# A two-layer block on one core: layer 0 with all transposed tokens kept, four value buffers, keys projected for several batches at once, and a new order on every engine

## The chip, the cores and the metric

One core of one Trainium2 chip. The metric is the device time of one execution in microseconds (us). TensorE (PE) multiplies, VectorE (DVE), ScalarE (ACT) and GpSimd (POOL) do the element work, and SyncE (SP) issues the DMAs. Matmul results land in eight PSUM banks of 512 float32 columns.

## What is computed

Eight batches of 256 tokens with 128 features pass two layers, each an attention-like branch plus a feed-forward branch on the normalised input. Cut to what matters:

```python
x = L0_attn_x                                   # (8, 256, 128)
xn = _layernorm(x)
# layer 0: attention, 16 heads of 8, 4 key/value heads, and a gated expert network
q, k, v = xn @ Wq + bq, xn @ Wk + bk, xn @ Wv + bv
attn = softmax(q k^T / sqrt(8)) ; out = (attn v) @ Wo + bo
ffn  = gates(top 2 of 8 of xn @ Wg) * (relu(xn @ w1) @ w2)
x = x + out + ffn
xn = _layernorm(x)
# layer 1: causal 4-tap convolution, a scan over the tokens of each batch with 16 states, and a
# 4-matrix network (128 -> 512 -> 512 -> 512 -> 128)
xs, z = split(xn @ W_in) ; xs = silu(conv(xs) + conv_b)
dt = softplus(xs @ W_dt + b_dt) ; B = xs @ W_x
h = h * exp(-exp(A_log) * dt) + B ; ys = sum(h) + D * xs      # per state, along the tokens
x = x + (ys * silu(z)) @ W_out + ternary_network(xn)
```

## The kernel before

**Layer 0** works batch by batch (8 batches `b`). The transposed, normalised tokens of a batch stand in one of two buffers `xnT`. `project` multiplies them with Wq and with Wk (tiled four times side by side, so that 128 rows come out, L457 and L460) into the two halves of one bank, ScalarE moves both out with their biases (`qk_out`, L521 and L522), GpSimd splits them into three bf16 parts (`qk_split`, L692 to L695), SyncE writes the parts to memory (`put`) and reads them back laid out by head (`fetch`, `stack`). The scores are made twice: `S` with tokens on the rows, for the maxima that VectorE takes (`M`, L589), and `A` with keys on the rows and the maxima folded in, for the exponentials of ScalarE (`E`, L548). There are 16 of each per batch. Two banks serve `S` and two serve `A`; for the last batch one of the latter goes to layer 1, so its `A` and `E` alternate. `S` uses the lower half of the array's rows and `A` the upper, and a pair placed together overlaps. `pv` multiplies the exponentials with the values (L357, four column tiles of 32 at a time); the values stand in one of two buffers `v_sb`. `heads`, `back` and `proj_out` finish the attention, `v_gate`, `ffn_in`, `ffn_out` and the small steps `G` on GpSimd make the value rows, the gate and the expert branch. `max_rows` transposes the maxima, `negated_maxima`, `maxima_split` and `rows` bring them into the operands of `A`.

**Layer 1** works on four groups `g` of 512 tokens. `x_in` (L933), the taps on ScalarE (L1015), the convolution on VectorE (L1142), `gate_x` and `gate_z` on ScalarE, `step_in` (L953) and `dt` (L1060) feed 32 decays `D` per group on ScalarE (L1088); VectorE runs 32 scans per group (L1163; one `scan` of the order is two of them), each on a row of B that `b` broadcasts (L869); GpSimd adds each scan to `acc` (L1218) and makes `y` (L1226), from which `out` starts (L970). `ffn`, `second` (L896) and `third` (L908) are the network, with `sil`, `gelu` and `hid` on ScalarE. Four buffer pairs `hb` stand between scans and additions, 31 buffers `da` between decays and scans. The start of `acc` for a group (L1210) waits for both `xs` tiles of that group.

**The order** is written out by hand for each engine in the table `ORDERS`, in which `S`, `A`, `scan` and so on are names of pieces, `3*M` is three of them, and the n-th use of a name is the n-th piece of its kind. Every engine runs its list in order; semaphores do the rest. `warm` is a pair of matmuls on ones (L451); there are 44 of them, and nobody reads what they make. A change of ScalarE's function set costs an `ACT_TABLE_LOAD`. The two layers overlap: layer 1 starts while the last two batches of layer 0 are still running.

## Time and profile before

| what | value |
|---|---|
| median of 3 runs | 371.86 us (370.92 to 372.0) |
| span of the profiled execution | 370.3 us |
| mean granted TensorE clock | 0.990 |
| busy: PE, DVE, ACT, POOL | 361.6, 303.1, 314.4, 238.0 us |
| instructions | 5874 |

The span counts from the first to the last instruction; the median lies 1.6 us above it. PE's busy time is modelled: matmuls overlap in the array, and the distance from the start of one to the start of the next is what one costs. A float32 matmul leaves two records, so x4 for `L457` in a row that covers one product of two parts is normal. POOL's 64% is an average over a first half in which it has little to do and a second in which it has no pause.

### The profile page before, as it was taken

The numbers are of one execution on the slowest core, as the hardware profiler recorded it, in microseconds if no ns is written. First come the engines' busy times: TensorE is split into PE (matmuls) and PEld (weight loads), VectorE is DVE, ScalarE is ACT, GpSimd is POOL, SyncE is SP. The second block draws the span as 40 slices with busy tenths as digits, with TensorE's granted clock in tenths as the row PEclk, the third lists the DMA queues.
The fourth block names the chain that finished last, engine by engine and source line by source line (L and its number), as shares of the span: only waits on it lengthen the run. The fifth ranks groups of instructions, "written<-read, shape, count | busy, mean of one in ns | idle before, by whom it ended". The sixth has DMA issues, their size and how long they took to land.

```text
span 370.3 us, 5874 instructions
## 1 busy us (share of the span) xinstructions
PE 361.6 (98%) x1810; PEld 185.9 (50%) x1810; DVE 303.1 (82%) x508; ACT 314.4 (85%) x540; POOL 238.0 (64%) x287
## 2 busy tenths in 40 slices
PE   7999999999999999999999999999999999999996
PEld 6757454546454553433324445465445464464546
DVE  4786879978788888579878768989999989998950
ACT  4934878886988887899998899999999999799870
POOL 2156504642527211342989673999999999999990
PEclk9999999999999999999969999999999999999999
DMA  6477282746265220220000000001000000000000
GB/s 217 125 145 147 93 200 35 174 143 120 58 110 123 43 55 2 52 85 0 1 21 3 1 0 2 0 0 48 5 0 21 0 3 28 1 2 1 0 28 28
DMA packets 29902, 19.63 MB, mean 53 GB/s; under 512 B 4496, under 2 KB 28848, under 8 KB 29616
## 3 DMA queue, kind: packets, MB, share of 16 engines
q1 hardware_dynamic: 29872, 19.26, 21.3%
q8 instruction: 14, 0.23, 0.3%
q14 instruction: 16, 0.13, 0.1%
HBM read 13.69 MB, written 5.37 MB: 51 GB/s over the span
## 4 chain that ended last, share of the span: by engine, by line
PE 68%; ACT 8%; DMA 2%; issue 2%; DVE 2%; SPq 0%; POOL 0%; ACTq 0%; DVEq 0%; POOLq 0%
PE bank L908 15%; PE bank L896 13%; PE bank L357 6%; PE bank L980 4%; PE bank L342 4%; ACT da L1088 3%; PE bank L869 3%; PE bank L885 3%; PE bank L886 3%; PE bank L953 3%; PE bank L933 3%; PE bank L388 2%; PE bank L328 2%; PE bank L396 2%; PE bank L970 2%; ACT pt L548 2%
## 5 line engine op out<-in xcount | busy, mean ns | idle before, releaser
L1218 POOL TENSOR_TENSOR acc<-acc,hb 128x512 f32<-128x512 f32 x128 | 158.1, 1273 | 11.6 <-DVE hb L1163 11.2
L1163 DVE TENSOR_TENSOR_SCAN hb<-da,bank 128x512 f32<-128x512 f32 x128 | 145.9, 1200 | 15.1 <-PE bank L869 9.1
L589 DVE TENSOR_REDUCE mx<-bank 128x2 f32<-128x512 f32 x128 | 83.1, 683 | 16.9 <-PE bank L328 14.4
L1088 ACT ACTIVATE da<-dt,nega 128x510 f32<-128x510 f32 x128 | 82.2, 713 | 0.2
L548 ACT ACTIVATE pt<-bank 128x512 f32<-128x512 f32 x128 | 71.2, 596 | 9.8 <-PE bank L342 8.7
L896 PE MATMUL bank<-sil,ld 128*128 128x512 f32 x128 | 59.1, 595 | 0.0
L908 PE MATMUL bank<-gelu,ld 128*128 128x512 f32 x128 | 58.5, 593 | 0.1
L342 PE MATMUL bank<-q_st,k_st 51*128 51x512 bf16 x128 | 42.2, 386 | 1.8 <-ACT pt L548 1.5
L328 PE MATMUL bank<-k_st,q_st 48*128 48x256 bf16 x240 | 38.9, 273 | 0.1
L896 PEld LDWEIGHTS bank<-sil,ld 128*128 128x128 f32 x128 | 24.3, 192 | 26.3 <-issue 25.7
L908 PEld LDWEIGHTS bank<-gelu,ld 128*128 128x128 f32 x128 | 23.8, 190 | 25.6 <-issue 24.7
L357 PE MATMUL bank<-pt,v_sb 128*32 128x512 f32 x256 | 35.4, 632 | 0.0
L342 PEld LDWEIGHTS bank<-q_st,k_st 51*128 51x128 bf16 x128 | 9.4, 93 | 38.3 <-ACT pt L548 25.5
L869 PE MATMUL bank<-b_parts,sel 96*128 96x512 bf16 x64 | 24.3, 393 | 0.4 <-DVE hb L1163 0.4
L1088 ACT ACT_TABLE_LOAD x18 | 23.1, 1283 | 0.3
L1142 DVE SCALAR_TENSOR_TENSOR xc<-bank,ld,xc 128x510 f32<-128x510 f32 (+2 forms) x24 | 17.6, 743 | 3.5 <-ACT xc L1015 2.9
L328 PEld LDWEIGHTS bank<-k_st,q_st 48*128 48x128 bf16 x240 | 15.5, 94 | 8.5 <-DVE mx L589 4.8
L692 POOL TENSOR_TENSOR qk_parts<-qk,qk_parts 128x512 bf16<-128x512 f32 x7 | 8.1, 1156 | 16.2 <-ACT qk_parts L522 16.2
L388 PE MATMUL bank<-xnT,w 128*128 128x256 f32 x64 | 17.3, 392 | 0.0
L933 PE MATMUL bank<-xnT,ld 128*128 128x512 f32 x32 | 16.7, 607 | 0.5 <-DVE xc L1142 0.3
L980 PEld LDWEIGHTS bank<-ld,gelu 128*128 128x128 f32 x128 | 15.8, 192 | 2.4 <-issue 2.1
L885 PE MATMUL bank<-xnT,ld 128*128 128x512 f32 x32 | 16.5, 598 | 0.0
(148 smaller groups left out, 534.0 us busy)
## 6 DMA issues: line engine op xcount, KB each, us to landing
q_st<-q_scr SPq DMA_DIRECT2D x8, 384.0 KB, 4.9
q_st<-q_scr SPq DMA_DIRECT2D x15, 192.0 KB, 3.8
ld<-in_pack SPq DMA_DIRECT2D x2, 1024.0 KB, 6.3
q_scr<-qk_parts SPq DMA_DIRECT2D x8, 192.0 KB, 2.1
k_st<-k_scr SPq DMA_DIRECT2D x15, 96.0 KB, 4.5
q_scr<-qk_parts SPq DMA_DIRECT2D x8, 128.0 KB, 2.1
out<-x SPq DMA_DIRECT2D x8, 128.0 KB, 1.9
ld<-in_pack SPq DMA_DIRECT2D x1, 968.0 KB, 5.4
```

The source lines that it names most:

```text
L328: last = mm(s_bank[n % 2][:, j * T:(j + 1) * T], q_st[b % 2][0:ROWS, 2 * pair + j, q * P:(q + 1) * P], k_st[b % 2][0:ROWS, 2 * pair // G, ...
L342: mm(st(b, n)[:, :], k_st[b % 2][HALF:, kv, kt * P:(kt + 1) * P], q_st[b % 2][HALF:, h0:h0 + 2, :].rearrange("r h n -> r (h n)"), start=Tr ...
L357: last = mm(pv_bank[kv * VW:(kv + 1) * VW, :], v_sb[b % 2][:, kt, kv, at:at + VW], pt[:, (4 * grp + kv) % 8, :], start=(grp == 0), stop=(g ...
L548: act(pt[:, n % 8, :], st(b, n)[:, :], ACT.Exp, scale=HD ** -0.5).then_inc(p_ok, 1)
L589: eng.tensor_reduce(mx[:, 2 * pair:2 * pair + 2, q], s_bank[n % 2][:, :].rearrange("p (h k) -> p h k", h=2), AX.X, ALU.max).then_inc(mx_ok, 1)
L869: mm(b_bank(g, s)[:, :], sel[:, s, :], b_parts[:, g % 2, :], start=True, stop=True).then_inc(b_ps, 1)
L896: last = mm(f_bank(g, c)[:, :], h1[:, k, c * P:(c + 1) * P], sil[:, k, :], start=(k == 0), stop=(k == KC - 1))
L908: last = mm(f_bank(g, c)[:, :], h2[:, k, c * P:(c + 1) * P], g2[:, k, :], start=(k == 0), stop=(k == KC - 1))
L980: last = mm(out_bank(g, q)[:, r], g3[:, k, r], w3[:, k, :], start=False, stop=(k == KC - 1 and q == out_last(g, q)))
L1088: act(da(n)[:, :, 1:T], dt[:, g % 2, c, :].rearrange("p (b n) -> p b n", b=GB)[:, :, 1:T], ACT.Exp, scale=nega[:, c, s:s + 1]).then_inc(da ...
L1163: eng.tensor_tensor_scan(hb[:, s % NPAIR, c, :], da(n).rearrange("p b n -> p (b n)"), b_bank(g, s)[:, :], 0.0, ALU.mult, ALU.add).then_inc ...
L1218: TT(acc[:, g % 2, c, :], acc[:, g % 2, c, :], hb[:, s % NPAIR, c, :], ALU.add).then_inc(add_ok, 1)
```

## The change

- The transposed tokens of all eight batches are kept: `xnT[b]` is now a slice of the buffer that layer 1 uses for its own transposed tokens. `xn` has two buffers in place of one, `v_sb` four in place of two (cleared one after another by `clear_values`).
- Keys are projected by `project_keys` for the batches (0), (1, 2, 3) and (4, 5, 6, 7) together: each batch's 32 key rows go to a column tile of their own of one bank. `project` makes the queries alone. Copying out, splitting and writing to memory are separate for queries (`q_out`, `split_q`, `put`) and keys (`k_out`, `split_k`, `put_keys`).
- Of the banks, the half `half0` of one is used by `xn_transposes`, `project` and keys of the last group, the half `half1` of another by `v_gate`, `max_rows`, `back` and `proj_out`, and `bB` by the expert branch and `heads`. Who has to have emptied a half before the next one writes it stands in tables of turns (`X_AFTER` to `H_AFTER`).
- The second part of x is 3 batches, not 2, and SyncE issues `head` before it and the constants before the expert weights.
- `scores`' first wait, the fetches and the row DMAs have semaphores for even and odd batches.
- All five lists of `ORDERS` are new.

```diff
+NV = 4
+KEYS = ((0,), (1, 2, 3), (4, 5, 6, 7))
+X_AFTER = "- q0 x1 x2 q1 q2 x5 x6"
+Q_AFTER = "x0 x3 x4 k2 q3 q4 q5 q6"
+KEYS_AFTER = "x7"
+V_AFTER = "- m0 m1 m2 m3 m4 m5 m6"
+M_AFTER = "v0 v1 v2 p1 p2 v5 p4 v7"
+T_AFTER = "v3 p0 v4 v6 p3 m7 h6 h7"
+P_AFTER = "t0 t1 t2 t3 t4 t5 t6 t7"
+F_AFTER = "- f0 f1 h1 h2 f4 h3 h4"
+H_AFTER = "f2 h0 f3 f5 f6 f7 p5 p6"
...
-    xnT = [sb(f"xnT_{p}", [P, T]) for p in range(2)]
-    xn = sb("xn", [P, TPB, P])
+    xnT = [t["xnT1"][:, b * T:(b + 1) * T] for b in range(NB)]
+    xn = [sb(f"xn_{p}", [P, TPB, P]) for p in range(2)]
...
-    v_sb = [sb(f"v_sb{p}", [P, TPB, NKV, VS + VW]) for p in range(2)]
+    v_sb = [sb(f"v_sb{p}", [P, TPB, NKV, VS + VW]) for p in range(NV)]
...
-    X_PARTS = ((0, TPB), (TPB, 3 * TPB), (3 * TPB, NT))
+    X_PARTS = ((0, TPB), (TPB, 4 * TPB), (4 * TPB, NT))
...
         def project(b):
             reached(eng, xnT_ok, b, 1, 1)
-            mm(bA[:, 0:T], wq[:, :], xnT[b % 2][:, :], start=True, stop=True)
+            emptied(eng, Q_AFTER, b)
+            mm(half0, wq[:, :], xnT[b], start=True, stop=True).then_inc(q_ps, 1)
             if b == 0:
-                mm(st_bank[0][:, 0:T], wkx[:, :], xnT[b % 2][:, :], start=True, stop=True)
-            mm(bA[:, T:2 * T], wk4[:, :], xnT[b % 2][:, :],
-               start=True, stop=True).then_inc(qk_ps, 1)
+                mm(st_bank[0][:, 0:T], wkx[:, :], xnT[b], start=True, stop=True).then_inc(kx_ps, 1)
+
+        def project_keys(j):
+            reached(eng, xnT_ok, KEYS[j][-1], 1, 1)
+            if j == 1:
+                eng.wait_ge(k_ok, 1)
+                eng.wait_ge(k_split, 1)
+            if j == 2:
+                emptied(eng, KEYS_AFTER, 0)
+            for i, b in enumerate(KEYS[j]):
+                last = mm(key_bank(j)[32 * i:32 * i + 32, :], wk4[:, 0:NKV * HD], xnT[b], start=True, stop=True)
+            last.then_inc(k_ps, 1)
...
-        def qk_out(b):
+        def q_out(b):
             eng.wait_ge(ld_cst, 16)
-            reached(eng, qk_ps, b, 1, 1)
-            reached(eng, split, b - 1, 3, 3)
-            reached(eng, scr_ok, b - 1, 16 * NSTK, 16 * NSTK)
-            for half, bias in ((0, bq_c), (1, bk_c)):
-                c = slice(half * T, (half + 1) * T)
-                if b > 0:
-                    act(qk[:, c], bA[:, c], ACT.Identity, bias=bias[:, 0:1])
-                last = act(qk_parts[:, 0, c], bA[:, c], ACT.Identity, bias=bias[:, 0:1])
-            last.then_inc(qk_ok, 1)
+            reached(eng, q_split, b - 1, 3, 3)
+            reached(eng, scr_ok, b - 1, 16 * NRUN, 16 * NRUN)
+            reached(eng, q_ps, b, 1, 1)
+            if b > 0:
+                act(qk[:, 0:T], half0, ACT.Identity, bias=bq_c[:, 0:1])
+            act(qk_parts[:, 0, 0:T], half0, ACT.Identity, bias=bq_c[:, 0:1]).then_inc(q_ok, 1)
...
-    vector="""ones moments inverse moments inverse v_out first_split M moments 5*M inverse M gate_sum M gate_norm 4*M
+    vector="""ones moments inverse moments clear_values inverse moments 2*first_split M v_out 3*M clear_values inverse
```

TensorE at the start of the program. L451 and L500 are the warm matmuls, L444 and L493 the transposes of batch 0, L457, L459, L460 and L507, L509, L519 the projections, L317 and L376 the first scores. Before:

```order
1 L451 MATMUL bank<-warm_in 128x256 x18
2 L444 MATMUL bank<-head,xn 128x128 x2
3 L451 MATMUL bank<-warm_in 128x256 x8
4 L457 MATMUL bank<-xnT,head 128x256
5 L459 MATMUL bank<-xnT,head 128x256
6 L460 MATMUL bank<-xnT,head 128x256
7 L388 MATMUL bank<-xnT,w 128x256 x2
```

After:

```order
1 L500 MATMUL bank<-warm_in 128x256 x40
2 L493 MATMUL bank<-head,xn 128x128 x2
3 L500 MATMUL bank<-warm_in 128x256 x8
4 L507 MATMUL bank<-xnT,head 128x256
5 L509 MATMUL bank<-xnT,head 128x256
6 L519 MATMUL bank<-xnT,head 32x256
7 L500 MATMUL bank<-warm_in 128x256 x2
```

Forty warm matmuls in place of 18 stand ahead of the first transpose, and the key product has 32 columns of weights.

TensorE around the last scores of batch 7. L342 and L403 are `A`, L357 and L418 `pv`, L953 and L1029 `step_in`, L869 and L944 `b`, L408 and L462 `back`, L414 and L469 `proj_out`, L896 and L971 `second`, L432 `heads`. Before:

```order
396 L869 MATMUL bank<-b_parts,sel 128x512
397 L953 MATMUL bank<-xs,ld 128x512 x2
398 L342 MATMUL bank<-q_st,k_st 128x512
399 L869 MATMUL bank<-b_parts,sel 128x512
400 L342 MATMUL bank<-q_st,k_st 128x512
401 L414 MATMUL bank<-cst,oT 128x128 x2
402 L342 MATMUL bank<-q_st,k_st 128x512 x2
403 L869 MATMUL bank<-b_parts,sel 128x512
404 L342 MATMUL bank<-q_st,k_st 128x512
405 L357 MATMUL bank<-pt,v_sb 32x512 x8
406 L869 MATMUL bank<-b_parts,sel 128x512 x2
407 L896 MATMUL bank<-sil,ld 128x512 x4
```

After:

```order
395 L403 MATMUL bank<-q_st,k_st 128x512
396 L418 MATMUL bank<-pt,v_sb 32x512 x4
397 L1029 MATMUL bank<-xs,ld 128x512 x2
398 L944 MATMUL bank<-b_parts,sel 128x512
399 L403 MATMUL bank<-q_st,k_st 128x512
400 L462 MATMUL bank<-head,on 128x128 x2
401 L403 MATMUL bank<-q_st,k_st 128x512
402 L418 MATMUL bank<-pt,v_sb 32x512 x4
403 L944 MATMUL bank<-b_parts,sel 128x512
404 L403 MATMUL bank<-q_st,k_st 128x512
405 L469 MATMUL bank<-cst,oT 128x128 x2
406 L418 MATMUL bank<-pt,v_sb 32x512 x4
```

A `pv`, a `step_in` and a `back` that stood ahead of the last four `A` now stand between them, and the last two `pv` no longer stand together.

VectorE at the turn from group 1's scans to group 2's. L1142 is the convolution and L1129 and L1205 the product for `zs`, both of group 3; L1125 and L1201 are the products for `sil` of group 2's network; L1163 and L1239 are scans. Before:

```order
215 L1142 SCALAR_TENSOR_TENSOR xc<-bank,ld,xc 128x2x253
216 L1163 SCALAR_TENSOR_TENSOR hb<-da,bank 128x512 x2
217 L1125 SCALAR_TENSOR_TENSOR sil<-bank,ld,sil 128x512
218 L1129 SCALAR_TENSOR_TENSOR zs<-zs,bank 128x512
219 L1125 SCALAR_TENSOR_TENSOR sil<-bank,ld,sil 128x512
220 L1163 SCALAR_TENSOR_TENSOR hb<-da,bank 128x512 x4
221 L1129 SCALAR_TENSOR_TENSOR zs<-zs,bank 128x512
222 L1125 SCALAR_TENSOR_TENSOR sil<-bank,ld,sil 128x512 x2
```

After:

```order
229 L1239 SCALAR_TENSOR_TENSOR hb<-da,bank 128x512 x6
230 L1201 SCALAR_TENSOR_TENSOR sil<-bank,ld,sil 128x512 x2
231 L1205 SCALAR_TENSOR_TENSOR zs<-zs,bank 128x512 x2
232 L1201 SCALAR_TENSOR_TENSOR sil<-bank,ld,sil 128x512
233 L1239 SCALAR_TENSOR_TENSOR hb<-da,bank 128x512 x2
234 L1201 SCALAR_TENSOR_TENSOR sil<-bank,ld,sil 128x512
235 L1239 SCALAR_TENSOR_TENSOR hb<-da,bank 128x512 x8
```

Five products in place of three stand ahead of the second pair of scans of group 2.

ScalarE at the turn from group 0's scans to group 1's. L1015 and L1091 write the tapped input, L1022 and L1098 are `zs` and L1109 `xs`, all of group 2; L1009 and L1085 are `sil` of group 1's network; L1118 makes the normalised rows of group 3; L1088 and L1164 are decays of group 1. Before:

```order
234 L1015 ACTIVATE xc<-bank,ld 128x512
235 L1088 ACT_TABLE_LOAD
236 L1088 ACTIVATE da<-dt,nega 128x2x255
237 L1015 ACTIVATE xc<-bank,ld 128x512
238 L1088 ACTIVATE da<-dt,nega 128x2x255
239 L1009 ACT_TABLE_LOAD
240 L1009 ACTIVATE sil<-bank,ld 128x512
241 L1022 ACTIVATE zs<-bank 128x512
242 L1009 ACTIVATE sil<-bank,ld 128x512
243 L1022 ACTIVATE zs<-bank 128x512
```

After:

```order
222 L1091 ACTIVATE xc<-bank,ld 128x512 x2
223 L1085 ACT_TABLE_LOAD
224 L1085 ACTIVATE sil<-bank,ld 128x512
225 L1118 ACTIVATE xn<-x,nmean,rstd 128x128 x4
226 L1085 ACTIVATE sil<-bank,ld 128x512
227 L1109 ACTIVATE xs<-xc 128x512
228 L1098 ACTIVATE zs<-bank 128x512 x2
229 L1085 ACTIVATE sil<-bank,ld 128x512
230 L1109 ACTIVATE xs<-xc 128x512
231 L1085 ACTIVATE sil<-bank,ld 128x512
232 L1164 ACT_TABLE_LOAD
233 L1164 ACTIVATE da<-dt,nega 128x2x255 x16
```

Two decays of group 1 that stood between the taps now stand behind all four `sil`, with one table load less. Over the whole program ScalarE's list holds 40 table loads in place of 49.

## Rows read from the trace of the kernel before

**Rows 1.** The page: the granted clock in 40 slices, tenths of full speed.

```profile
PEclk9999999999999999999969999999999999999999
```

**Rows 2.** Stretch, us, busy PE, PEld, DVE, ACT, POOL, clock, DMA share, GB/s.

```profile
154.40:188.10 33.70, 32.14 (x122) 11.86 (x124) 27.16 (x35) 33.15 (x55) 19.05 (x19) 0.96 0.12 38
...
184.00:186.00 2.00, 1.24 (x6) 0.48 (x5) 2.00 (x3) 2.00 (x4) 1.94 (x4) 0.83 0.00 0
186.00:192.00 6.00, 5.85 (x22) 1.41 (x22) 3.42 (x7) 5.35 (x9) 5.44 (x6) 0.50 0.12 33
...
229.00:361.60 132.60, 132.60 (x463) 67.74 (x461) 119.47 (x117) 125.53 (x171) 130.72 (x112) 1.00 0.03 10
```

**Rows 3.** Timeline of PE: start us, us, what, count, at five places.

```profile
35.02 0.39 PE L342 MATMUL bank<-q_st,k_st 51*128 51x512 bf16 x1
...
153.05 1.45 PE L953 MATMUL bank<-xs,ld 128*128 128x512 f32 x3
...
186.92 0.61 PE L342 MATMUL bank<-q_st,k_st 51*128 51x512 bf16 x1 [0.15 <-ACT pt L548]
...
216.05 1.88 PE L933 MATMUL bank<-xnT,ld 128*128 128x512 f32 x4
...
361.97 1.95 PE L970 MATMUL bank<-wout_half,y 128*128 128x128 f32 x16
```

**Rows 4.** Timeline of PE, the start.

```profile
1.36 3.62 PE L451 MATMUL bank<-warm_in 128*128 128x256 bf16 x18 [1.36 <-DVE warm_in L558]
...
5.99 1.04 PE L451 MATMUL bank<-warm_in 128*128 128x256 bf16 x8
...
7.30 0.59 PE L459 MATMUL bank<-xnT,head 128*128 128x256 f32 x2
7.73 0.59 PE L460 MATMUL bank<-xnT,head 128*128 128x256 f32 x2
```

**Rows 5.** Timeline of DVE: statistics of part 2 of x, batch 0's split.

```profile
4.55 0.87 DVE L569 BATCH_NORM_STATS2 bst<-x_sb 128x6 f32<-128x128 f32 x4
...
10.03 0.88 DVE L662 SCALAR_TENSOR_TENSOR qk_rest<-bank,cst,qk_parts 128x256 f32<-128x256 f32 x2
```

**Rows 6.** DMA issues: KB each, median us to landing.

```profile
q_st<-q_scr SPq DMA_DIRECT2D x15, 192.0 KB, 3.8
...
x_sb<-in_x SPq DMA_DIRECT2D x1, 640.0 KB, 6.5
```

**Rows 7.** Timeline of ACT: group 0's `dt`, the last `E`.

```profile
154.44 1.28 ACT L1060 ACT_TABLE_LOAD   x1
...
187.56 0.60 ACT L548 ACTIVATE pt<-bank 128x512 f32<-128x512 f32 x1
```

**Rows 8.** The chain that ended last: start us, us, what.

```profile
109.70 1.85 PE bank L357 x16
...
187.53 3.57 PE bank L357 x16
191.10 0.97 PE bank L869 x2
```

**Rows 9.** Groups by line: busy us, mean ns of one, idle before.

```profile
L1088 ACT ACTIVATE da<-dt,nega 128x510 f32<-128x510 f32 x128 | 82.2, 713 | 0.2
```

**Rows 10.** Timeline of POOL in the second half.

```profile
228.96 2.51 POOL L1218 TENSOR_TENSOR acc<-acc,hb 128x512 f32<-128x512 f32 x2
231.93 8.65 POOL L1218 TENSOR_TENSOR acc<-acc,hb 128x512 f32<-128x512 f32 x7 [0.46 <-DVE hb L1163]
...
359.13 2.49 POOL L1226 TENSOR_TENSOR y<-acc,zs 128x512 f32<-128x512 f32 x2
```

**Rows 11.** Timeline of DVE: group 2's second pair of scans first.

```profile
275.83 4.54 DVE L1163 TENSOR_TENSOR_SCAN hb<-da,bank 128x512 f32<-128x512 f32 x4
```

**Rows 12.** Timeline of ACT: `zs`, then the second `sil` of group 2.

```profile
273.89 0.59 ACT L1022 ACTIVATE zs<-bank 128x512 f32<-128x512 f32 x1
274.44 0.69 ACT L1009 ACTIVATE sil<-bank,ld 128x512 f32<-128x512 f32 x1
```

More of the change, by code:

```diff
@@ L119 @@
-    gpsimd="""ones G qk_split G biased 6*G qk_split maxima_split 6*G biased 2*G qk_split maxima_split 6*G maxima_split
-        qk_split 3*G biased 7*G maxima_split qk_split 8*G maxima_split qk_split 7*G maxima_split G qk_split G
-        constants 7*G shifted maxima_split 8*G maxima_split split 2*start 3*add start 9*add split 9*add start 7*add
-        shifted 4*add 2*y start 9*add split 23*add start 2*y 2*add start 2*add split add start 27*add 2*y 32*add 2*y""",
+    sync="""x_in head x_in constants0 ffn_weights x_in put_keys 3*put 2*put_keys fetch stack 2*put_keys put put_keys
+        2*put fetch put 3*rows stack 2*put fetch rows loads 2*rows 2*put put_keys stack put loads fetch put_keys put
+        put_keys 2*put 3*rows fetch put stack put rows put loads 2*rows fetch put stack 2*put 3*rows fetch stack
+        3*rows loads stack 3*put fetch 4*rows stack 2*rows 2*b_rows out b_rows 3*out b_rows 4*out landed""",
@@ L123 @@
+    gpsimd="""biased ones biased G split_k split_q 7*G split_q maxima_split 6*G split_k 2*G maxima_split split_q 3*G
+        split_q 4*G maxima_split G split_q 7*G biased maxima_split 9*G split_q maxima_split 8*G maxima_split 7*G
+        split_q G shifted maxima_split 4*G constants 4*G maxima_split 2*start split 5*add split 3*add start 20*add
+        shifted add start 2*add y add y start 3*add start 8*add split 21*add 2*y 8*add start split 5*add start 21*add
+        2*y 30*add 2*y""",
 )
@@ L214, in layer0, with score_bank, score_free, group_of @@
     LAST = NB - 1
+    NS3 = LAST * NH
     def head_bank(b):
-        return bA if b < LAST - 1 else bC
+        return bB if b < LAST - 1 else bX
     def st(b, n):
         return st_bank[n % 2 if b < LAST else 0]
+    def score_bank(b, n):
+        return s_bank[n % 2]
+    def score_free(eng, b, n):
+        reached(eng, mx_ok, b, NH, n - 1)
+    def group_of(b):
+        return next(j for j, batches in enumerate(KEYS) if b in batches)
+    def key_bank(j):
+        return half0 if j == 2 else st_bank[1][:, 0:T]
+    EMPTIED = dict(x=((xnT_ok, 1),), q=((q_ok, 1),), k=((k_ok, 1),), v=((v_ok, 1), (srt_ok, TPB)), m=((negm_ok, 1),),
+                   t=((oT_ok, 1),), p=((x1_ok, 1),), h=((on_ok, 1),), f=((y_ok, 1),))
+    def emptied(eng, before, n):
+        name = before.split()[n]
+        if name == "-":
+            return
+        for signal, per in EMPTIED[name[0]]:
+            eng.wait_ge(signal, per * (int(name[1:]) + 1))
+        if name == "q0":
+            eng.wait_ge(q_split, 1)
+            eng.wait_ge(kx_ok, 2)
     def x_part(b):
@@ L302, in ffn_weights @@
             eng.dma_start(w12[:, :], a["w12"]).then_inc(ld_ffn, 16)
-        return dict(x_in=x_in, head=head, constants0=constants0, ffn_weights=ffn_weights, put=put, fetch=fetch, rows=rows,
+        return dict(x_in=x_in, head=head, constants0=constants0, ffn_weights=ffn_weights, put=put, put_keys=put_keys, fetch=fetch, rows=rows,
                     stack=stack, loads=loads)
@@ L1283, in program @@
         early = early_buffers(sb)
[L1284 removed]
+        t["hb"], t["dt"], t["xnT1"] = early["hb"], early["dt"], early["xnT1"]
         with ExitStack() as only0:
```

326 lines of the change are left out of this document (172 added, 154 removed).

## Prediction

> **What bounds the kernel now.** The profiled execution spans 370.3 us and the median is 371.86, so 1.56 us lie around the span. I read the page's rows by slices first. The clock row [rows 1] has one slice at six tenths, a little past the middle, and full speed everywhere else. Then PE's timeline at the places where the program changes character [rows 3] cuts the span into five: 35.02 us to the first `A`; 118.03 to the first `step_in` of layer 1 (153.05), in which PE's pieces follow each other; 33.87 to the last `A` (186.92); 29.13 to the first `x_in` of group 2 (216.05); 145.92 from there to the last group's `out0` (361.97), and 8.3 behind it.
>
> The table of stretches [rows 2] says who is full in each. In 154.4 to 188.1 ScalarE is busy 33.15 of 33.70 us: the last exponentials and the decays of group 0 lie one behind the other, and PE waits for them now and then (busy 1.24 of 2 us in 184 to 186, granted clock 0.83 there). Then the clock is 0.50, the lower of its two levels (1.2 of 2.4 GHz), from 186 to 192, exactly where both last `pv` lie: 16 records took 3.57 us, and 1.85 in the middle of the program [rows 8]. That cost is on the path, because behind the last `A` PE is full again. In 229.0 to 361.6 GpSimd is busy 130.72 of 132.60 us and PE 132.60: the additions end in `y` at 361.62 [rows 10], `out0` starts at 361.97. Two engines bound this part together, so a gain on PE alone brings nothing there.
>
> **The change, part by part.**
>
> *Key products.* A product of 256 columns costs 0.43 us from start to start [rows 4]; before there are eight of them for `S`'s keys, 3.44 us. After there are three groups of one, three and four column tiles. Column tiles placed together already stand in the program: 16 records of `pv`, that is two pieces of four tiles with 512 columns, take 1.85 us [rows 8], 0.93 each, 0.46 with 256 columns; with 0.08 for entering and leaving it is 0.54 a group. Bounds: 0.43 (no such cost) and 1.72 for four tiles that don't run together (4 x 0.43). I take 0.54, since `pv` is the same form. Five of the eight products (batches 3 to 7) stood behind the first `A`, on the full stretch of PE; one group of four replaces them: 2.15 - 0.54 = **1.6 us less**. The other two groups lie at the start, where PE waits and fills with warm matmuls. The wider split on GpSimd and ScalarE's ten copies fewer lie beside PE's work and cost nothing there.
>
> The Trainium skill ("TensorEngine Tiling (Array Packing)", Key Properties) says that a change of tiling mode drains TensorE. No row here shows a drain by itself. By that rule, with the 0.16 us by which a record of 0.59 outlasts its distance of 0.43 [rows 4] paid once in and once out, my estimate would be 0.3 us less gain.
>
> *Start.* The first 18 warm matmuls take 3.62 us (0.20 each), and once the clock is up eight take 0.87 (5.99 to 6.86, 0.11 each) [rows 4]. Twenty-two more ahead of the first transposes cost at most 22 x 0.11 = 2.4 us behind 4.98, which puts these at about 7.4 in place of 5.72. Against this, PE's wait for the `head` load goes, `head` and the constants are issued earlier, and ahead of the first `A` PE's list is stretched with warm matmuls that fill waits. VectorE now has the statistics of the third part of x ahead of batch 0's split, which started at 10.03 [rows 5]. That part is issued near 3 us, and a load of 640 KB took 6.5 [rows 6], so it lands near 9.5 (it is 512 KB now); eight statistics at 0.22 [rows 5] and their means end near 12. Batch 0's queries and keys then come some 2 us later, but their `A` stands at 35. What could be late is batch 1: its first `S` needs the joint keys of batches 1 to 3. The tokens of batch 3, their keys' product, copy, split and three writes come first; counting these in the lists I place the fetch near 25, and with its 3.8 us [rows 6] the keys land at 28.9, about when the first scores that read them are due. Bounds for the first `A`: 34.0 (the waits for the loads go and nothing is late) and 38. I take **35.0, no change**.
>
> *First `A` to `step_in`.* 118.0 less the 1.6 of the keys, less 0.4 for a `proj_out` (four records of 128 columns) that now stands behind the last `A`: **116.0**. The other banks and buffers in turns change who waits, but waits here are of the kind of the 0.15 us ahead of the last `A` [rows 3]; a dozen more or fewer of them bound it at -2 to +2, and I take nothing.
>
> *`step_in` to the last `A`.* ScalarE bounds it and its set of work there is the same (a table load 1.28, an `E` 0.60 [rows 7]). **33.9, no change.** PE has more between its last `A`'s now: a `pv`, a `step_in` and a `back`, about 0.93 + 0.86 + 0.22 us. These fill ScalarE's time, not the path's.
>
> *Last `A` to `x_in`.* Before, two `pv` and two `b` run here at half clock: 3.57 + 0.97 us [rows 8] in place of 1.85 + 0.48. If PE is kept busy between the last `A`'s the clock stays up: 2.2 less. One `pv` (0.93) and one `b` (0.22) are ahead of the last `A` now, a `proj_out` (0.44) comes behind it: 0.7 less. The last `pv` must wait for the last `E`, which started 0.64 us behind its `A` and took 0.60 [rows 3, 7]; the products ahead of it last 0.66, so 0.7 more. 29.1 - 2.2 = **26.9**. Bounds: 26.2 (no wait) and 29.1 (the half clock stays).
>
> *`x_in` to the last `out0`.* Before, the first addition of group 1 starts 12.9 us behind `x_in` (228.96 - 216.05) [rows 3, 10], because two decays stand between the taps. After, all decays come behind the last `sil`. PE feeds it with 12 products of 512 columns at 0.86 (twice 0.43) and two `b` of 0.22, 10.8 us; then `sil` 0.6, table load 1.28 [rows 7], a decay 0.71 [rows 9], a scan 4.54/4 = 1.14 [rows 11], and 0.4 from engine to engine: **14.9**. From there GpSimd's work is the same: 132.66 us to the end of `y` (361.62) less its own idle 1.35 is 131.3. One new wait comes: group 2's second pair of scans stood 59.8 us behind `x_in` [rows 11]; now five products are ahead. Its second `sil` is ready 58.4 behind `x_in` [rows 12], the third `sil` and the products of both `zs` come four PE products later: 58.4 + 3.5 = 61.9, the first result at 63.0, while GpSimd, which before took the result of 60.9 at once, is free at 60.9 + 2.0 (its later start) - 1.35 (its idle) = 61.6. With a product for `sil` between this pair and the next (0.5) that is **1.9**. 14.9 + 131.3 + 1.9 = **148.1**, against 145.9. Bounds: 144.2 (no later start, no new wait) and 150. ScalarE's nine table loads fewer (11.5 us) and PE's gain don't count here, GpSimd's chain ends last.
>
> *Behind `out0`*: 8.3, as before.
>
> Sum: 35.0 + 116.0 + 33.9 + 26.9 + 148.1 + 8.3 = 368.2 of profile, and with 1.56 **369.8 us**.
>
> **The rivals.**
>
> *B, the half clock stays.* ScalarE still sets the distance of the last `A`'s, and PE still waits for it. In the profile the clock fell behind a stretch in which PE was busy 1.24 of 2 us [rows 2]; the 2.0 us of added work stand nearer to the end than those gaps, which may be elsewhere now. Then the 2.2 are not won: 369.8 + 2.3 = 372.1, no measurable change. The Trainium skill ("TensorE: Matmul & The Clock Gate", Part 1) says that TensorE falls back to half speed after idling. The trace agrees in this place, but also ran at half speed while PE was mostly busy.
>
> *C, GpSimd's chain doesn't grow.* If the first addition comes as early as before, or the five products before the second pair find their data sooner, up to 2.2 go: 367.6. For it: VectorE is busy 119.47 and ScalarE 125.53 of these 132.60 us [rows 2], so both could come earlier. Against it: PE's products come one every 0.86 us and the lists are fixed.
>
> *D, a late start, slower than before.* Place: the first scores of batch 1. They wait for the keys of batches 1 to 3 to be projected, copied, split in three parts, written (three DMAs), and read back. Behind them on PE stand all scores that feed VectorE's maxima. It decides once the fetch lands later than 28.9 us; each us costs one. The 2 us of delay of the split on VectorE, if they reach it, and one more for the third batch's transposes, give 3.4: 373.2. For it: the third part of x lands near 9.5 and VectorE's queue stands on it. Against it: before, these waits were covered by warm matmuls.
>
> *E, the end.* PE has no work left while `y` is awaited if GpSimd alone is late by 2 us; before, `third` ended just there. If the clock falls then, the last 5.4 us of PE's work double: 375.2.
>
> *F, the change's key tiles don't run together*: (1.72 - 0.54) on the path and 1 more at the start: 372.0.
>
> **Chances.** Forecast 0.38, B 0.22, C 0.17, D 0.15, E 0.05, F 0.03. A measurement of this kernel can tell 0.3% from no change, that is below 370.7 or above 373.0 us. The forecast's own range (368.6 to 371.0) lies mostly below: 0.31 faster, 0.07 same. C all faster; B 0.02 faster, 0.16 same, 0.04 slower; D 0.02 same, 0.13 slower; E slower; F 0.02 same, 0.01 slower. Sum: faster 0.50, same 0.27, slower 0.23. The range takes in C with its bound and D, and leaves E and the far side of D out: 366.8 to 374.2.
>
> **What would show it.** First `A` at 34 to 36 us, and PE's idle before batch 1's scores put down to a DMA if D. One group of four key tiles taking about 0.54 behind the first `A`. First `step_in` at 151. No slice under nine tenths in the clock row past the middle, and the last `pv` at about 0.93 us; if it takes 1.8, B. GpSimd's first `acc<-acc,hb` of group 1 at 14.9 behind `x_in`, its idle in front of group 2's second pair 1.4 and more; if GpSimd's time from first addition to `y` is 131, C. `third` should end before `out0` starts; a long `out` at the end would be E. What would make all this wrong is a wait in the 116 us of PE's pieces: buffers of values, the banks in turns and the new order of the maxima change every piece's neighbours there, and I have priced them at nothing.

## The result

The changed kernel takes 385.89 us (median of 4 runs, 381.58 to 387.27) against 371.49 for the kernel before (370.92 to 372.0): a ratio of 1.037, 95% interval 1.031 to 1.043. It is slower by 14.4 us. The prediction was 369.8 us with a range of 366.8 to 374.2, so it was wrong in sign and far outside its range. The profiled execution spans 383.1 us; against the forecast for it, 368.2, 14.9 us have to be found.

The same five places on PE as in [rows 3], in the profile of the changed kernel (start us, us, line and operation, what ended the idle before it):

```profile
35.41 0.38 PE L403 MATMUL bank<-q_st,k_st 51*128 51x512 bf16 x1
...
160.95 1.45 PE L1029 MATMUL bank<-xs,ld 128*128 128x512 f32 x3
...
194.88 0.39 PE L403 MATMUL bank<-q_st,k_st 51*128 51x512 bf16 x1
...
223.39 1.09 PE L1009 MATMUL bank<-xnT,ld 128*128 128x512 f32 x2
...
373.11 2.84 PE L1046 MATMUL bank<-wout_half,y 128*128 128x128 f32 x16 [3.55 <-POOL y L1303]
375.74 4.59 PE L1056 MATMUL bank<-ld,gelu 128*128 128x128 f32 x32
```

They give this table, in us:

| stretch | before | forecast | after | miss |
|---|---|---|---|---|
| start to first `A` | 35.0 | 35.0 | 35.4 | +0.4 |
| to the first `step_in` | 118.0 | 116.0 | 125.5 | **+9.5** |
| to the last `A` | 33.9 | 33.9 | 33.9 | 0.0 |
| to group 2's `x_in` | 29.1 | 26.9 | 28.5 | +1.6 |
| to the last group's `out0` | 145.9 | 148.1 | 149.7 | +1.6 |
| behind it | 8.3 | 8.3 | 10.0 | +1.7 |

Two thirds of the miss lie in one stretch, the 118 us of PE's pieces that I had called full and priced for its keys alone. The page of the changed kernel shows the place (busy tenths and granted clock in 40 slices of 9.6 us):

```profile
PE   8999999959999999999999999999999999999967
...
PEclk9999999985999999999999999999999999999998
```

The ninth slice of PE is half empty, and the clock is low in the same slice and the next. The slice at six tenths that [rows 1] has past the middle is gone, and the very last slice, at eight tenths, is new. By stretches, with the columns of [rows 2]:

```profile
80.00:82.00 2.00, 1.98 (x16) 0.52 (x15) 2.00 (x7) 1.55 (x3) 0.00 (x0) 1.00 0.87 217
82.00:84.00 2.00, 0.08 (x4) 0.00 (x0) 0.62 (x4) 0.22 (x1) 0.81 (x4) 1.00 0.94 352
84.00:86.00 2.00, 0.00 (x0) 0.00 (x0) 0.00 (x0) 0.00 (x0) 0.00 (x0) 0.50 1.08 182
86.00:90.00 4.00, 3.87 (x20) 1.08 (x20) 1.69 (x3) 1.99 (x4) 0.00 (x0) 0.50 0.11 18
90.00:94.00 4.00, 3.65 (x15) 2.19 (x16) 3.51 (x9) 1.80 (x4) 0.20 (x1) 0.50 0.00 0
```

From 84 to 86 none of the four compute engines works at all, while the DMA engines are busy throughout (the share of 1.08 counts them as full) and the clock has fallen to its lower level, 1.2 GHz. It stays there until 94.2, 10.2 us in all, though PE is busy again from 86.1. What the DMA engines do can be read from the timeline of SyncE's queue:

```profile
77.94 0.51 SPq L330 DMA_DIRECT2D q_st<-m_parts  x1
78.50 0.58 SPq L289 DMA_DIRECT2D q_scr<-qk_parts  x1
79.11 0.43 SPq L348 DMA_DIRECT2D ld<-in_pack  x1
79.65 1.14 SPq L330 DMA_DIRECT2D q_st<-m_parts  x2
80.88 0.53 SPq L309 DMA_DIRECT2D k_st<-k_scr  x1
```

and PE's timeline has behind the gap, first of all, an `A`:

```profile
86.13 0.58 PE L403 MATMUL bank<-q_st,k_st 51*128 51x512 bf16 x1 [4.05 <-issue]
```

`L348` is `loads`, 1 MB of weights for layer 1, and `L330` is `rows`, 8 KB each, the maxima that the first `A` of batch 3 needs. The change's SyncE list has `rows put loads 2*rows`. The load landed at 85.22 us; the last two rows, issued at 79.65 and 80.26, landed at 84.66 and 86.04. The profile names no releaser for this stop (`<-issue`); that it is the last row follows from its landing 0.09 us ahead of the `A`, and the two experiments that move this load bear it out. Of the 24 row DMAs the trace gives the landing times so (all of the changed kernel; in the kernel before the longest is 2.2 us):

```profile
DMA to landing us min/median/max: 1.8/1.8/5.8
```

Two more rows stand behind a load: that of 559 KB issued at 46.57 landed after 3.6 us, and the rows issued 0.6 and 1.2 us behind it took 3.1 and 3.0 us. PE waits 0.47 us there, up to the first `A` of batch 1 at 50.81.

### The profile page after: what moved, and what is told of

Its sections match the earlier page's. It is cut to its first block, busy times and chain, and to the rows that moved or that the text cites. A ratio compares the mean times of both kernels' runs of the same rounds, so it can differ in the third digit from the quotient of the medians.

```text
span 383.1 us, 5851 instructions
## 1 busy us (share of the span) xinstructions
PE 367.0 (96%) x1810; PEld 185.0 (48%) x1810; DVE 303.2 (79%) x514; ACT 299.0 (78%) x521; POOL 231.7 (60%) x293
## 4 chain that ended last, share of the span: by engine, by line
PE 49%; issue 26%; ACT 8%; DVE 7%; POOL 7%; DMA 3%; SPq 0%; POOLq 0%; ACTq 0%; DVEq 0%
PE bank L418 6%; PE bank L403 5%; POOL acc L1295 4%; DVE hb L1239 4%; PE bank L983 4%; PE bank L446 3%; PE bank L387 3%; PE bank L971 3%; ACT da L1164 3%; PE bank L500 3%; PE bank L454 2%; PE bank L1056 2%; PE bank L1009 2%; PE bank L960 2%; DMA q_scr<-qk_parts 2%
## 5 line engine op out<-in xcount | busy, mean ns | idle before, releaser
L1239 DVE TENSOR_TENSOR_SCAN hb<-da,bank 128x512 f32<-128x512 f32 x128 | 145.4, 1200 | 10.1 <-ACT da L1164 5.7
L1164 ACT ACTIVATE da<-dt,nega 128x510 f32<-128x510 f32 x128 | 81.1, 711 | 0.1
L971 PE MATMUL bank<-sil,ld 128*128 128x512 f32 x128 | 59.6, 594 | 0.3 <-ACT gelu L1145 0.3
L983 PE MATMUL bank<-gelu,ld 128*128 128x512 f32 x128 | 58.4, 593 | 0.7 <-ACT gelu L1145 0.7
L403 PE MATMUL bank<-q_st,k_st 51*128 51x512 bf16 x128 | 42.9, 393 | 5.9 <-issue 4.8
L387 PE MATMUL bank<-k_st,q_st 48*128 48x256 bf16 x240 | 41.1, 281 | 0.5 <-DVE mx L654 0.4
L418 PE MATMUL bank<-pt,v_sb 128*32 128x512 f32 x256 | 35.0, 619 | 0.0
L971 PEld LDWEIGHTS bank<-sil,ld 128*128 128x128 f32 x128 | 23.6, 190 | 22.6 <-issue 21.8
L403 PEld LDWEIGHTS bank<-q_st,k_st 51*128 51x128 bf16 x128 | 9.4, 94 | 37.5 <-ACT pt L613 19.7
L944 PE MATMUL bank<-b_parts,sel 96*128 96x512 bf16 x64 | 24.0, 382 | 0.2 <-DVE hb L1239 0.2
L1056 PEld LDWEIGHTS bank<-ld,gelu 128*128 128x128 f32 x128 | 17.2, 202 | 3.7 <-issue 3.5
L1056 PE MATMUL bank<-ld,gelu 128*128 128x128 f32 x128 | 17.4, 284 | 0.0
L1152 ACT ACTIVATE gelu<-bank,ld 128x512 f32<-128x512 f32 x16 | 10.5, 686 | 7.9 <-PE bank L983 7.7
L1009 PE MATMUL bank<-xnT,ld 128*128 128x512 f32 x32 | 16.6, 614 | 0.1
```

Of the source, the lines that this page charges most:

```text
L387: last = mm(score_bank(b, n)[:, j * T:(j + 1) * T], q_st[b % 2][0:ROWS, 2 * pair + j, q * P:(q + 1) * P], k_st[b % 2][0:ROWS, 2 * pair // ...
L403: mm(st(b, n)[:, :], k_st[b % 2][HALF:, kv, kt * P:(kt + 1) * P], q_st[b % 2][HALF:, h0:h0 + 2, :].rearrange("r h n -> r (h n)"), start=Tr ...
L418: last = mm(pv_bank[kv * VW:(kv + 1) * VW, :], v_sb[b % NV][:, kt, kv, at:at + VW], pt[:, (4 * grp + kv) % 8, :], start=(grp == 0), stop=( ...
L971: last = mm(f_bank(g, c)[:, :], h1[:, k, c * P:(c + 1) * P], sil[:, k, :], start=(k == 0), stop=(k == KC - 1))
L983: last = mm(f_bank(g, c)[:, :], h2[:, k, c * P:(c + 1) * P], g2[:, k, :], start=(k == 0), stop=(k == KC - 1))
L1056: last = mm(out_bank(g, q)[:, r], g3[:, k, r], w3[:, k, :], start=False, stop=(k == KC - 1 and q == out_last(g, q)))
```

## Experiments

All times are compared with the changed kernel's 385.89 us and with runs of the kernel before on the same chip.

**Two loads behind the rows.** The SyncE list of the changed kernel:

```diff
-... fetch rows loads 2*rows 2*put ...  rows put loads 2*rows fetch put stack
+... fetch 3*rows loads 2*put ...  rows put 2*rows fetch loads put stack
```

> The changed kernel with the 1 MB weight loads of batches 1 and 3 issued behind the three row DMAs (and behind the fetch) and not between them. Theory (in the changed kernel the row DMAs of 8 KB issued at 79.65 and 80.26 us landed at 84.66 and 86.04, behind the load issued at 79.11 that landed at 85.22, and the first A of batch 3 started at 86.13): that A starts near 82, PE's stop of 4.05 us and the 10.2 us of half clock behind it go, 8.5 to 10 us less, about 376.5. Rival (the joint keys or the banks in turns hold batch 3 up): the stop stays, and the time is within 1 us of 385.9.

Measured: 382.73 us (379.46 to 385.19); the profiled execution spans 377.7, the shortest of four. In it batch 3's first `A` starts at 83.58, and the stop at 82 is gone. But the gain of the median is 3.2 us (4.6 without the longest of the four executions), not 9, so the expected time is missed, and another stop stands earlier, in PE's timeline:

```profile
58.71 0.39 PE L403 MATMUL bank<-q_st,k_st 51*128 51x512 bf16 x1 [2.37 <-ACT pt L613]
```

ScalarE's timeline has just ahead of it:

```profile
57.23 0.47 ACT L576 ACTIVATE qk<-bank,cst 128x256 f32<-128x256 f32 x1 [3.18 <-DMA q_scr<-qk_parts]
```

`L576` is ScalarE's copy of batch 4's queries. It waits for the last `put` of batch 3's queries, issued at 51.79 behind a load and the `stack` of batch 2 and landed at 57.07; the exponentials stand behind it on ScalarE, `A` behind those on PE. The two longest of the four executions (384.17 and 385.19) have mean clocks of 0.982 and 0.978, the two shorter ones 0.995 and 0.987. So the clock was low for longer in the long ones; that it fell at this stop is not shown, since in the one trace it stays at 1.00 here.

**The mirror image in the kernel before.**

```diff
-... 3*put fetch loads 3*rows 3*put ...
+... 3*put fetch rows loads 2*rows 3*put ...
```

> The kernel before with one weight load moved from behind a fetch to between the first and the second row DMA of batch 3, as the change has it. Theory: the last two rows land behind the load, the first A of batch 3 starts 3 to 4 us later than 81.0, and the whole is 3.5 us longer, up to 8 if the clock halves there. Rival (something of the new kernel alone makes the stop): no change, 371.5.

Measured: 375.92 us against 371.28, ratio 1.0125 (1.011 to 1.014), 4.6 us slower. In PE's timeline the release is named:

```profile
83.69 0.58 PE L342 MATMUL bank<-q_st,k_st 51*128 51x512 bf16 x1 [2.69 <-DMA q_st<-m_parts]
```

A stop of 2.69 us and 3.41 us of half clock (from 83.5), from one moved DMA. So the stop goes when the load is taken away from the rows, and comes, with its releaser named, when a load is put there.

**The stop filled.** 36 matmuls with zero weights stand ahead of batch 3's first `A`:

```diff
+            if n >= NWARM:
+                eng.wait_ge(warm_ok, 2)
+                for _ in range(2):
+                    mm(pv_bank[:, 0:256], zeros[:, :], warm_in[:, P:3 * P], start=False, stop=False)
+                return
```

> The changed kernel with 18 pairs of 128x256 bf16 matmuls with zero weights (nothing is added by them) ahead of the first A of batch 3, where PE stands for 4 us. Theory: the A still starts near 86, the half clock of 10.2 us doesn't come, and the time is 4.5 to 5.5 us less, about 381. Rival (the stop alone costs the 9 us): no change, 385.9.

Measured: 381.71 us (381.13 to 381.85), 4.2 us less, a little under what was expected, and the four executions agree within 0.7 us, where the changed kernel's differ by 5.7. PE's timeline:

```profile
81.71 4.10 PE L483 MATMUL bank<-warm_in,zeros 128*128 128x256 bf16 x36
85.74 0.39 PE L384 MATMUL bank<-q_st,k_st 51*128 51x512 bf16 x1
```

and by stretches:

```profile
86.00:90.00 4.00, 3.49 (x33) 1.23 (x28) 3.55 (x7) 2.88 (x6) 0.00 (x0) 1.00 0.04 7
```

The `A` comes hardly earlier (85.74 for 86.13), but the clock stays at 1.00. The profiled executions can be split: from the first `A` to the first `step_in` this kernel takes 122.23 us (35.34 to 157.57), the changed one 125.54, and e11_second_load_earlier below, which has no stop, 118.03. So the stop costs 4.2 us there and the low clock 3.3, 7.5 together; the 4.2 us between the medians contain executions in which the clock was low for longer.

**Two decays early again,** as in the kernel before, against the change's ScalarE and VectorE lists:

```diff
-... hid 2*taps sil normalise sil ... 16*D      ... 2*mul 2*zm 2*mul 4*scan
+... hid taps D taps D sil normalise sil ... 14*D   ... 2*mul 2*zm scan 2*mul 3*scan
```

> The changed kernel with two decays of group 1 between its taps and their scans ahead of two sil products, as before the change. Theory: GpSimd's first addition of group 1 comes 13 us behind x_in and not 15.3, and since GpSimd's chain ends last, the time is 2 us less, 383.9. Rival (the later waits of GpSimd take it up, or ScalarE's further table load costs it): no change within 0.5 us.

Measured: 385.63 us. The first addition does come 13.0 us behind `x_in` (235.97 - 222.99), but `x_in` to `out0` takes 150.7 us, not less than 149.7: at 276.56 GpSimd waits 1.95 us in place of 0.54. The rival holds; the late first addition was not what this stretch hung on. The order of layer 0 is the changed kernel's, and its stop is there again: PE stands 4.22 us and the clock is low for 3.4 us (86.8 to 90.2), where the changed kernel's profiled execution has 4.05 and 10.2.

**All three loads at their old places.**

```diff
-... 3*rows stack 2*put fetch rows loads 2*rows 2*put put_keys stack put loads fetch ...
+... 3*rows loads stack 2*put fetch 3*rows loads 2*put put_keys stack put fetch ...
-... rows put loads 2*rows fetch put stack ...
+... rows put 2*rows fetch loads put stack ...
```

> The changed kernel with all three weight loads of layer 0 issued at the places of the kernel before: one behind the rows of batch 0 (near 34 us, not 46), one behind the rows of batch 1 (near 48), one behind the fetch of batch 4. Moving two of them alone left two 1 MB loads within 5 us of each other, a put issued at 51.79 landed at 57.07, and ScalarE's query copy, which waits for it, held the exponentials and PE by 2.4 us. Theory (the queue of loads is the cause of both stops): no stop over 1 us in layer 0, first A of batch 3 at 81 to 82, first step_in at 152 to 153.5, time 374 to 376 and the runs within 1.5 us of each other. Rival (the query copy waits for its put whatever the loads do): the stop near 56 us stays, 378 to 383.

Measured: 383.68 us (382.58 to 387.59), the rival's stop and a time just above its range. In the profiled execution, the longest of the six (385.5 us of span), ScalarE's copy waits for its `put` 5.55 us and PE stops for 4.74, and then the clock stays halved for 17 us:

```profile
60.41 0.61 PE L403 MATMUL bank<-q_st,k_st 51*128 51x512 bf16 x1 [4.74 <-ACT pt L613]
```

The load of 968 KB at 47.50 stands ahead of the whole row of small writes now, and the change's list has the third `put` behind the `stack`. Old places in a new list are not the old order.

**The products of `y` last.** In the last group PE adds the network's products (32 records) first, and those of `y` (16) last:

```diff
+            if g == NG - 1:
+                if n < KC + 1:
...
+                        last = mm(out_bank(g, q)[:, r], g3[:, k, r], w3[:, k, :],
+                                  start=(k == 0 and q == out_first(g, q)), stop=False)
+                    return
+                reached(eng, y_ok, g, CI, CI)
...
+                        last = mm(out_bank(g, q)[:, r], y[:, c, r], wo[:, c, :], start=False,
+                                  stop=(c == CI - 1 and q == out_last(g, q)))
```

> As e5_loads_as_before, and in the last group the products of the network (32 records) ahead of those of y (16 records) in PE's list and in the bank. Theory (at the end PE stands 3.6 us for y, the clock halves, and the network's 3.6 us of products come behind y): behind y only the 16 records remain, at full clock; 4.5 to 5.5 us less than e5_loads_as_before. Rival (the network's products wait for their own operand, or the residual and the output DMAs set the end): less than 2 us.

Measured: 377.75 us (376.89 to 380.40), 5.9 less than 383.68 and a little more than expected. The profiled executions show it at the place itself: from the start of `y`'s products to the end of the span it is 10.0 us in e5_loads_as_before (375.50 to 385.5) and 4.8 here. In the changed kernel PE stood 3.55 us for `y` and then ran at half clock (first section). Here it is busy to the end:

```profile
370.15 3.73 PE L1044 MATMUL bank<-ld,gelu 128*128 128x128 f32 x32
373.72 2.00 PE L1053 MATMUL bank<-wout_half,y 128*128 128x128 f32 x16
```

**The pair of scans ahead of `zs`.**

```diff
-... 3*scan 2*mul 2*zm mul scan mul 4*scan
+... 3*scan 2*mul scan 2*zm 2*mul 4*scan
```

> As e6_y_last, and on VectorE the second pair of scans of group 2 behind two products for sil, ahead of both products for zs. Theory (this wait of GpSimd, 1.80 us at 285.8 in the changed kernel, is the cost of the new order of the second half): GpSimd takes the pair 1 to 2 us earlier, 1 to 1.8 us less. Rival (the pair waits for its decays or its row of B, or GpSimd loses the time again before the end): within 0.4 us of e6_y_last.

Measured: 379.79 us (378.25 to 380.38), no gain. GpSimd's wait of 1.80 us goes, and two others of 1.25 and 1.27 us come instead. VectorE waits for a row of B from PE there:

```profile
292.32 2.33 DVE L1263 TENSOR_TENSOR_SCAN hb<-da,bank 128x512 f32<-128x512 f32 x2 [1.44 <-PE bank L944]
```

So in this trace PE's list holds it, not the order on VectorE; no run moves PE's `b` to test that.

**The same turn in the kernel before.** The edit of e6_y_last.

> The kernel before with the same turn of the last group's output products as e6_y_last. There PE finishes third when y is ready, so the network's products (3.59 us) would stand ahead of y's: if GpSimd's y is what ends last, they fit only into time in which PE waits, and PE had none there. Theory (both engines end together at 361.9): the sum on PE stays the same and the gain is under 1 us: 371. Rival (PE's list has slack of its own in the second half that this order uses): up to 3.6 us less, 368.

Measured: 371.12 us against 371.60, ratio 0.999 (0.997 to 1.001): no difference, as the theory has it. PE's work is the same, and there it never stood for `y`.

**SyncE's list sorted.** The first and the third load stand as in e5_loads_as_before. Further, batch 3's third `put` goes ahead of the `stack`, and the second load goes down the list, from 47.50 to 67.36 us:

```diff
-... 3*rows stack 2*put fetch rows loads 2*rows 2*put put_keys stack put loads fetch put_keys put
+... 3*rows loads stack 2*put fetch 3*rows 2*put put_keys put stack fetch put_keys put
-... fetch put stack put rows put loads 2*rows fetch put stack
+... fetch put stack put loads rows put 2*rows fetch loads put stack
```

> The changed kernel with SyncE's list alone altered: as in e5_loads_as_before, and further the third put of batch 3's queries ahead of the stack of batch 2, and the second weight load 18 us later. In e5_loads_as_before that put was issued at 51.51, behind 288 KB of stack and a load, landed at 58.76, and ScalarE's query copy waited for it 5.55 us with the exponentials behind it. Theory (a small DMA behind a large one in the queue holds up what needs it): the put is issued near 50 with no load ahead within 15 us and lands within 2.5 us, ScalarE's wait is under 1 us, no half clock in layer 0, first A of batch 3 at 81 to 82, first step_in at 152.5 to 153.5, and with the tail as it is 374.5 to 376. Rival (the put is held by the copies and splits ahead of it, not by the queue): the stop near 56 us stays and the time is over 380.

Measured: 384.28 us, and a miss, though the stop at 56 us is gone: `A` of batch 2 starts at 63.70, earlier than before the change (64.66). The wait has moved to the load that I had put off:

```profile
75.13 0.20 ACT L1175 ACTIVATE f_half<-ld 128x4 f32<-128x4 f32 x1 [6.75 <-DMA ld<-in_pack]
```

The change prepares layer 1's constants on ScalarE at 68 us (`decay_rates`), and these come with the second load.

**The sorted queue and `y` last together.**

> As e9_queue_sorted, and the last group's network products ahead of those of y. Theory: the stops in layer 0 and the stand at the end together are what made the changed kernel slower, so this is 369.5 to 371.5, at or a little under the kernel before (371.6). Rival (the new orders cost PE more in layer 0 by themselves): 373 or more with no stop over 1 us in the trace.

Measured: 378.74 us (377.99 to 380.31). The turn at the end gives 5.5 us here too (384.28 - 378.74). The expected time is missed, because the stop of e9_queue_sorted is left: PE stands 5.38 us up to 76.71, 5.91 up to 76.92 there.

**The second load 6 us earlier,** against e10_queue_and_y_last:

```diff
-... put_keys 2*put 3*rows fetch put stack put loads rows put ...
+... put_keys 2*put 3*rows loads fetch put stack put rows put ...
```

> As e10_queue_and_y_last, with the second weight load issued behind the rows of batch 2 (near 61 us) and not 6 us later: in e10_queue_and_y_last it landed at 74.90, and ScalarE's preparation of layer 1's constants, which the change does at 69 us, waited 6.2 us for it, with the exponentials behind. Both stops of the changed kernel (the put at 56 us, the rows at 82 us) are away as well. Theory (all that the change loses in layer 0 is waits behind the three weight loads in SyncE's queue): no stop over 1 us, no half clock before the end, first A of batch 3 at 81 to 82, first step_in at 152.5 to 154, time 370.5 to 372.5, level with the kernel before. Rival (the new orders cost PE more by themselves, or each place for the loads meets some other wait): a stop of over 1.5 us at another place, or 374 and more.

Measured: 371.54 us (370.44 to 372.58, 12 runs) against 370.97, ratio 1.002 (1.000 to 1.004). Against the changed kernel that is 14.3 us less, from the place of four entries in one queue and one turn at the end. Its page shows no gap:

```profile
PE   8999999999999999999999999999999999999996
...
PEclk9999999999999999999999999999999999999999
```

**The warm pairs behind the first `A` left out.** The trace of e11_second_load_earlier answers where the keys' gain is: first `A` to first `step_in` is 118.03 us (34.93 to 152.96), to the hundredth what it was before. Projections take 3.37 us, not 5.12, as forecast. But ten warm pairs stand in it (2.82 us) where before there were four (1.10).

```diff
-NWARM = 44
+NWARM = 34
...
-... S 2*warm xn_transposes warm A S A S 2*warm A S warm A S 2*warm A S A S warm project_keys warm S
+... S xn_transposes A S A S A S A S A S A S project_keys S
```

> As e11_second_load_earlier, without the ten warm matmul pairs that the change has behind the first A (the kernel before has four there); nobody reads what they make. Between the first A and the first step_in that kernel takes 118.02 us, as long as the kernel before (118.03), although its projections take 3.37 us in place of 5.12; its ten warm pairs take 2.82 us there, the four of before 1.10. Theory (the six pairs more are what took the keys' gain): first step_in 1 to 2.8 us earlier, 369 to 370.5, under the kernel before. Rival (the pairs stand where PE waits for ScalarE or VectorE anyway): within 0.5 us of e11_second_load_earlier.

Measured: 372.4 us, ratio 1.002 (1.000 to 1.004). No gain. By stretches, this kernel:

```profile
36.00:38.00 2.00, 1.90 (x11) 0.70 (x10) 2.00 (x5) 2.00 (x5) 0.39 (x2) 1.00 1.02 286
38.00:40.00 2.00, 1.96 (x13) 0.57 (x16) 1.89 (x4) 2.00 (x5) 0.00 (x0) 0.59 1.21 142
40.00:45.00 5.00, 5.00 (x30) 1.33 (x34) 3.30 (x8) 1.95 (x5) 2.32 (x5) 0.50 0.52 125
```

and e11_second_load_earlier:

```profile
38.00:40.00 2.00, 2.00 (x18) 0.93 (x17) 1.82 (x4) 1.78 (x4) 0.00 (x0) 1.00 1.23 155
40.00:45.00 5.00, 5.00 (x42) 1.57 (x42) 4.41 (x10) 2.69 (x6) 2.32 (x5) 1.00 0.44 111
```

Without them PE follows ScalarE and VectorE, both nearly full from 36 to 40, and the clock falls for 6.8 us, although the profile has PE busy for 1.90 and 1.96 of 2 us just before. From the first `A` to the first `step_in` it is 118.61 us, 0.6 more. The pairs do cover waits, as the rival says, and they keep the clock up as well.

## Why the prediction was wrong

**The step that failed** is the one on the 118 us from the first `A` to the first `step_in`. I wrote that "the other banks and buffers in turns change who waits" and took nothing, with bounds of -2 to +2. The bounds came from waits of 0.15 us, but the change also moved loads of 0.6 to 1 MB within SyncE's list, and I never priced these. The loads themselves stand in the page of the kernel before:

```profile
ld<-in_pack SPq DMA_DIRECT2D x2, 1024.0 KB, 6.3
```

If a row of 8 KB issued half a microsecond or more behind such a load lands when the load does, it lands 5 to 6 us after its issue; that estimate was open to me, and the trace has 5.0 and 5.8. The forecast asked only what a fetch at 28.9 us would meet. The mechanism of rival D was of the right kind (a DMA that lands late, with all scores behind it), at the wrong place, and its price left out that the clock halves at a stop: with 4.05 us of stop the stretch takes 7.5 us more than without (125.54 against 118.03 us in e11_second_load_earlier).

**First `A`:** 35.41 for 35.0. The first transposes came at 7.73 (7.4), batch 0's split started at 11.52 (near 12); neither mattered. Right.

**Key products:** the group of four tiles takes 0.57 us (0.54):

```profile
40.74 0.64 PE L519 MATMUL bank<-xnT,head 128*32 128x256 f32 x8
41.31 0.39 PE L500 MATMUL bank<-warm_in 128*128 128x256 bf16 x2
```

Rival F is out. That the 1.6 us don't appear in the end is a second miss: I counted the 44 warm pairs as unchanged and didn't see that six more of them stand behind the first `A`, on the stretch that I called full. What the ten pairs there hide, e12_no_warm_behind_first_A shows, is waits, so the gain was not there to take: the stretch is not full everywhere.

**`step_in` to the last `A`:** 33.93 us, 33.9. Right, ScalarE sets it.

**Last `A` to `x_in`:** the half clock did go. The last `pv`, at 195.96, takes 0.99 us to the next piece, not 1.8, and rival B is out. The forecast gain of 2.2 us was eaten, for the larger part, by waits for `gelu` that I hadn't looked for, 0.28 and 0.73 us, the longer in front of `third`:

```profile
207.97 2.41 PE L983 MATMUL bank<-gelu,ld 128*128 128x512 f32 x5 [0.73 <-ACT gelu L1145]
```

PE came earlier to products whose operands ScalarE made no earlier. I had also counted one `b` fewer behind the last `A`; there are eight in both traces. The term was mis-sized: 0.6 us of gain, not 2.2; what remains of the difference wasn't followed up.

**`x_in` to `out0`:** GpSimd's first addition comes at 15.3 (14.9), and its waits behind that are

```profile
275.91 4.95 POOL L1295 TENSOR_TENSOR acc<-acc,hb 128x512 f32<-128x512 f32 x4 [0.54 <-DVE hb L1239]
...
287.58 2.50 POOL L1295 TENSOR_TENSOR acc<-acc,hb 128x512 f32<-128x512 f32 x2 [1.80 <-DVE hb L1239]
290.46 5.00 POOL L1295 TENSOR_TENSOR acc<-acc,hb 128x512 f32<-128x512 f32 x4 [0.38 <-DVE hb L1239]
```

and 0.53 us at 303, 3.25 in all where I had 1.9. The stretch is 1.6 us over: 0.4 from the first addition, 1.0 from there to the end of `y` (134.2 us for 133.2), and 0.25 from `y` to `out0`, which my sum left out. The main wait came at its place and near its size, 1.80 us in front of group 2's second pair, but by some luck: the pair's scans started 62.9 us behind `x_in` (I had 61.9, with 58.4 read as the end of the second `sil` where [rows 12] has its start) and GpSimd was free 62.4 behind it (61.6), and the two errors mostly cancel. What I drew from it was not right: removing the late start or the wait gave nothing (e4_decays_early, e7_scan_early); in the second the trace names PE's rows of B, in the first VectorE reaches the scans of the new wait 0.65 us later (275.27 for 274.62) with no wait over 0.46 us of its own in the 20 us before, and what made it later was not followed up.

**Behind `out0`:** rival E happened, with a chance of 0.05. I had priced GpSimd 2.2 us later and left PE's end where it was, which says by itself that PE would stand. It stood 3.55 us and ran at 1.2 GHz for 3.4 us, and the 32 records of the network, 3.74 us before, took 4.59. The price was 1.7 us and not 5.4. The cure is worth more than the clock: with `y`'s products last, 5.9 us (e6_y_last against e5_loads_as_before), because the network's products fill the wait.

The changed kernel's four executions lie between 381.58 and 387.27 us, and their mean clocks follow: 0.991 at 381.58, 0.982 at 384.94, 0.978 at 386.84 and 387.27. So the spread goes with how long the clock was low, and e3_stop_filled, where it is low only at the end, has 0.7 us of it. One program can have different lengths of it: e4_decays_early, whose order in layer 0 is the same, had 3.4 us at this stop in its profiled execution, and this one 10.2. What decides between them stays open. None of the twelve kernels is faster than the one before; the change, with its queue in order, is level with it.

## What to carry to other kernels

In a hand-ordered DMA queue the bulk loads are the first thing to look at when the order changes: for each one, list the small DMAs issued in the next 5 us and who waits for them, and the instructions that wait for the load itself. A stop of TensorE can cost more than its length where the clock falls with it: in the traces here from 1.2 to 2.8 times, and less than its length where the clock stayed up. Where two engines end together, a forecast that makes one of them later must also say what the other does in the meantime, and put there work that doesn't need the late result.
